# A paged-attention stage: the order of the key loads, a semaphore for the new keys, and their scaling moved from VectorE to GpSimd

## The chip, the cores and the metric

The kernel runs on one core of one Trainium2 chip. The metric is the device time of one execution in microseconds (us). TensorE, VectorE, ScalarE and GpSimd are the compute engines (PE, DVE, ACT and POOL in the profile); SyncE (SP) only issues DMAs.

## The reference

Two layers, each a conditioning block followed by a feed-forward block with LoRA experts and a residual. The block that matters here is the attention of the second layer: 64 batches (B) of 32 new tokens (S), 32 query heads, 8 key heads (HK), head size 128 (P), and 16 pages (NPP) of 32 cached keys each per batch.

```python
q = _rope(_rmsnorm(q, q_norm_w), pos); k = _rope(_rmsnorm(k, k_norm_w), pos)
kc = k_cache[block_table].reshape(bsz, L, HK, D)      # 512 cached keys per batch
k_all = jnp.concatenate([kc, k], axis=1)              # and 32 new ones
scores = jnp.where(valid, einsum('bqhd,bkhd->bhqk', q, k_all) * SCALE, -1e30)
o = einsum('bhqk,bkhd->bqhd', softmax(scores), v_all)
```

## The kernel before

The program goes through five stages: prologue, first feed-forward, `project` (queries, keys and values), `attention`, `output_projection`, then the second feed-forward. `project` stores turned but unnormalised keys (`qk_t`) and, apart from them, the reciprocal norms (`inv_d`, 8 heads x 32 tokens per batch). So the 32 new keys of a batch must be multiplied by their reciprocals in SBUF before they can be used.

`attention` is one software pipeline over units; a unit is one key head of one batch, so a batch has 8. The helper `turns` unrolls the first 12 steps and then loops over 16 units (two batches) at a time. At step u each engine works on several units at once; `live(n)` marks the part of the step that belongs to unit u - n. I number the steps of a batch 0 to 7, step 0 being the one at which its first unit enters. For a batch b the order is:

- VectorE, step 1 (`live(1)`): waits for all keys of b (`s_kp[q]`), multiplies the new ones by `inv` (line 1454), counts `s_fixed`. This stands ahead of the last split of batch b - 1 in the same step.
- VectorE, steps 2 and 3 (`live(2)`, `split`): the high half of the keys of the first two heads (line 1444, waits for `s_fixed`), then the low half (line 1447), which counts `s_lo`. In each step the splits stand ahead of the masked scores and row maxima of an older unit (line 1467).
- TensorE, step 4 (`live(4)`): the scores of unit 0 (line 1354), which wait for `s_lo`. TensorE works strictly in this order: scores, turning of probabilities (1363), products with cached values (1388), and once in four steps those with new values (1395). The last 1395 of batch b - 2 stands in step 0 of batch b and counts `s_nw`.
- GpSimd, once a batch: waits for `s_nw` of batch b - 2, copies the factors of b (line 1330), copies its row numbers (1311), issues four indirect DMAs that gather the cached values of b (1305).
- SyncE, once a batch: queries, then, when the key buffer is free (`s_lo` of the last split of b - 2), the reciprocals (1236), 16 pages (1245), the new keys (1248), then new values (1253) and the store of results.

All key buffers (`kt`), value buffers and so on are double: `q` is the parity of the batch. Batches 0 and 1 are prepared by `project`: its VectorE part multiplies their new keys (line 1031) after waiting for all 17 loads of the batch (line 1030), and only then starts the attention's own VectorE program, which computes the row numbers for the first gathers.

Of the kernel before, what the change touches and what calls it, by code (L numbers as in the profile page):

```python
# [19 lines left out]
ALU = mybir.AluOpType  # L20
# [3 lines left out]
P = 128  # L24
B, S, L = 64, 32, 512
# [5 lines left out]
HQ, HK, D = 32, 8, 128  # L31
REP = HQ // HK
PAGES, PSIZE, NPP = 64, 32, 16
# [672 lines left out]
def wait_apart(eng, sem_passed, *waits):  # L706


    for sem, v in waits:
        wait(eng, sem, v)  # L710
    eng.sem_inc(sem_passed, 1)
# [84 lines left out]
def project(nc, block, sems, ps, dram, cst, xh, xl, tables, spare, wcol, shared, qk_t, v_own, k_t, sums_d, ksums_d, inv_d, w, keys, first, early, spent):  # L796
# [6 lines left out]
    with ExitStack() as ctx:  # L803
        sb = lambda n, s, d=F32: ctx.enter_context(nc.sbuf_tensor("pr_" + n, s, d))
        sem = lambda n: sems.enter_context(nc.semaphore("pr_s_" + n))
        kt, qk, s_kp, s_qk = keys
        s_ev, s_xlo, s_tab = first
        turned = sb("turned", [P, 2, 2, 512])
        sums = sb("sums", [P, 512])
# [55 lines left out]
        @block.sync  # L865
        def _(e):
            src = bass.AP(tensor=dram["itok_Bx16_0_63"].tensor, offset=0, ap=[[0, 1], [1, 2 * NPP]])
            e.dma_start(page[0:1, :], src).then_inc(s_page, 16)

            def store(i, j):  # L870
                c, p, q = chunk(i, j), pair(i, j), j // 2 % 2
                high, n, _ = split(j)
                for half in range(2):
                    for head in range(2):
                        at = c * P + (2 * head + high) * S
                        cols = slice(at, at + S) if static(at) else bass.ds(at, S)
                        e.dma_start(qk_t[n * NT:(n + 1) * NT, half * H:(half + 1) * H, cols].rearrange("b d x -> d b x"),
                                    turned[head * H:(head + 1) * H, q, half, :].rearrange("p (b x) -> p b x", b=NT)).then_inc(s_qs[q], 16)

            def step(i, j, u, live):  # L880
                if live(0) and j % NT == 0 and not (static(u) and u == 0):
                    w.load(e, chunk(i, j) + 1, chunk(i, j) + 1)
                if live(2) and j % 2 == 1:
                    e.wait_ge(s_rot, pair(i, j - 2) + 1)
                    store(i, j - 2)
                if live(4) and (j - 4) % PER == PER - 1:
                    it = i + (j - 4) // PER
                    e.wait_ge(s_cs, it + 2)
                    for n in range(T // 512):
                        rows = slice(it * 8, it * 8 + 8) if static(it) else bass.ds(it * 8, 8)  # L890
                        out = ksums_d[n:n + 1, :, :] if key(u - 4) else sums_d[n:n + 1, rows, :]
                        e.dma_start(out.rearrange("o h x -> (o h) x"), sums[n * 32:n * 32 + 8, :]).then_inc(s_cd, 16)

            steps(e, step)
            for c, t, n in values:
                n -= QKT
                if t == 0 and c + 1 < chunks:
                    w.load(e, c + 1, c + 1)
                e.wait_ge(s_stage, n + 1)
                staged, s_stored, _ = staging(n)  # L900
                e.dma_start(v_own[t * P:(t + 1) * P, (c - NQU) * 512:(c - NQU + 1) * 512], staged).then_inc(s_stored, 16)
                b, place = divmod(n, NPP)
                if n == 0:
                    e.wait_ge(s_page, 16)
                if place == 2:
                    for q in range(2):
                        e.wait_ge(*rotated[q])
                    e.dma_start(kt[:, b, NPP, :],
                                qk_t[b:b + 1, :, HK * P:HK * P + HK * S].rearrange("o d x -> (o d) x")).then_inc(s_kp[b], 16)
                    e.dma_start(qk[:, b, :], qk_t[b:b + 1, :, 0:HK * P].rearrange("o d x -> (o d) x")).then_inc(s_qk[b], 16)  # L910
                if place % PPT == 0:
                    at = b * NPP + place
                    pages = nc.values_load_multi_w_load_instructions(
                        page[0:1, at:at + PPT], engines=[mybir.EngineType.SP], min_val=0, max_val=PAGES - 1,
                        skip_runtime_bounds_check_because="the block table holds numbers of pages of the cache")[1]
                e.dma_start(kt[:, b, place, :], k_t[bass.ds(pages[place % PPT] * P, P), :]).then_inc(s_kp[b], 16)
                if n == 4:
                    e.wait_ge(s_cd, 64 * (QKT // PER + 1))
                    e.dma_start(roots[:, :], sums_d.rearrange("n h x -> (n h) x")).then_inc(s_ss, 16)
                    e.dma_start(roots_k[:, :], ksums_d.rearrange("n g x -> (n g) x")).then_inc(s_ss, 16)  # L920
                if n == 14:
                    e.wait_ge(s_inv, 1)
                    for m in range(T // 512):
                        e.dma_start(inv_d[m * NT:(m + 1) * NT, :, :].rearrange("b g s -> g b s"),
                                    roots_k[m * HK:(m + 1) * HK, :].rearrange("g (b s) -> g b s", s=S)).then_inc(s_id, 16)
                if n == 17:
                    e.wait_ge(s_id, 64)
                    e.dma_start(sums[:, :], inv_d[0:2, :, :].rearrange("(o b) g s -> o (b g s)", o=1).broadcast_to([P, 512])).then_inc(s_id, 16)
                if c == chunks - 1 and t == 6:
                    e.wait_ge(w.s_lo, chunks * KB)  # L930
                    early.load(e, dram)
# [53 lines left out]
        def _(e):  # L985
# [41 lines left out]
            e.wait_ge(s_id, 80)  # L1027
            for b in range(2):
                new = kt[:, b, NPP, :]
                e.wait_ge(s_kp[b], 16 * (NPP + 1))  # L1030
                e.tensor_tensor(new, new, sums[:, b * HK * S:(b + 1) * HK * S], ALU.mult).then_inc(s_fixed, 1)
            e.wait_ge(s_fixed, 2)

# [142 lines left out]
def attention(nc, block, sems, ps, dram, cst, k_t, qk_t, v_own, o_t, inv_d, ri_d, keys, results, early, projected, late):  # L1176
# [7 lines left out]
    PER = 2 * UB  # L1184
    CB = T // 512
    QU = REP
    NPG = NPP + 1
    W = 2 * P
    SC = 1.0 / math.sqrt(D)
    with ExitStack() as ctx:  # L1190
        sb = lambda n, s, d=F32: ctx.enter_context(nc.sbuf_tensor("at_" + n, s, d))
        sem = lambda n: sems.enter_context(nc.semaphore("at_" + n))
        kt, qk, s_kp, s_qk = keys
        w_raw, o_raw, ri_b, s_w, s_or, s_on, s_ot = results
        s_proj, s_stage, s_rot, rotated, stores, own_stored = projected
        tiles, own = (NQU + HK // REP) * NT, HK // REP * NT
# [31 lines left out]
        def _(e):  # L1228
# [4 lines left out]
            def load_keys(b, q):  # L1233

                scales = inv_d[bass.ds(b, 1), :, :] if not isinstance(b, int) else inv_d[b:b + 1, :, :]
                e.dma_start(inv[:, q, :], scales.rearrange("o g s -> o (g s)").broadcast_to([P, HK * S])).then_inc(s_kp[q], 16)

                for n in range(0, NPP, PPT):
                    at = b * NPP + n
# [3 lines left out]
                        skip_runtime_bounds_check_because="the block table holds numbers of pages of the cache")  # L1243
                    for k in range(PPT):
                        e.dma_start(kt[:, q, n + k, :], k_t[bass.ds(numbers[k] * P, P), :]).then_inc(s_kp[q], 16)
                cols = slice(HK * P, HK * P + HK * S)
                src = qk_t[bass.ds(b, 1), :, cols] if not isinstance(b, int) else qk_t[b:b + 1, :, cols]
                e.dma_start(kt[:, q, NPP, :], src.rearrange("o d x -> (o d) x")).then_inc(s_kp[q], 16)

            def load_v(b, q):  # L1250
                own = v_own[bass.ds(b * S, S), :] if not isinstance(b, int) else v_own[b * S:(b + 1) * S, :]
# [50 lines left out]
        def _(e):  # L1302
# [5 lines left out]
            def indices(b, q):  # L1308

                cols = slice(b * KC, (b + 1) * KC) if isinstance(b, int) else bass.ds(b * KC, KC)  # L1310
                e.tensor_copy(idx[:, q, :], rows[:, cols]).then_inc(s_idx, 1)

            e.wait_ge(s_rot, NQU * NT // 2)
            e.wait_ge(s_rows, 1)
            for q in range(2):
# [4 lines left out]
            e.memset(v_new[0][:, :, :], 0.0).then_inc(s_cleared_rs, 1)  # L1320
            e.wait_ge(s_proj, tiles)
            e.memset(v_new[1][:, :, :], 0.0).then_inc(s_cleared_rs, 1)
            e.wait_ge(s_factors, 1)
            for q in range(2):
                e.tensor_copy(factor[:, q, :], factors[q][:, 0:HK]).then_inc(s_factor, 1)
            with e.Fori(0, B // 2 - 1) as i:
                for q in range(2):
                    b = i * 2 + q
# [2 lines left out]
                    indices(b + 2, q)  # L1331
                    wait_apart(e, s_passed[0], (s_idx, b + 3))
                    gather_values(q)

        @block.tensor
        def _(e):
# [67 lines left out]
        def _(e):  # L1404
# [14 lines left out]
            def step(i, j, u, live):  # L1419
# [14 lines left out]
                        ins.then_inc(s_ri, 1)  # L1434
                def split(jj):
                    q, g, w = (jj // UB) % 2, jj % UB, (jj // 2) % 2
                    if g == 0 and not (isinstance(u, int) and jj < PER):
                        e.wait_ge(s_fixed, i * 2 + jj // UB - 1)
                    elif g == 0:
                        e.wait_ge(s_kp[q], 16 * NPG)  # L1440
                    two = lambda x: x[:, w, :, :].rearrange("p x (n k) -> p n x k", k=PSIZE)
                    raw = kt[:, q, :, (g // 2) * 2 * PSIZE:(g // 2 + 1) * 2 * PSIZE].rearrange("p n (x k) -> p n x k", k=PSIZE)
                    if g % 2 == 0:
# [3 lines left out]
                        e.tensor_tensor(two(k_lo), raw, two(k_hi).bitcast(F32), ALU.subtract).then_inc(s_lo, 1)  # L1447


                if live(1) and (j - 1) % UB == 0 and not (isinstance(u, int) and j - 1 < PER):  # L1450
                    q = (j - 1) // UB % 2
                    new = kt[:, q, NPP, :]
                    e.wait_ge(s_kp[q], (i + (j - 1) // PER) * 16 * (NPG + 1) + 16 * NPG)
                    e.tensor_tensor(new, new, inv[:, q, :], ALU.mult).then_inc(s_fixed, 1)
                if live(2) and not (isinstance(u, int) and u == 5):
                    split(j - 2)
                if isinstance(u, int) and u == 4:
# [268 lines left out]
def build(nc, dram, out_t):  # L1726
# [12 lines left out]
    with ExitStack() as ctx:  # L1739
# [12 lines left out]
        kt = shared[:, 0:KT_SIZE].rearrange("p (q n x) -> p q n x", q=2, n=NPP + 1)  # L1752
        qk = shared[:, KT_SIZE:KT_SIZE + QK_SIZE].rearrange("p (q x) -> p q x", q=2)
        pair = lambda n: [ctx.enter_context(nc.semaphore(f"{n}{q}")) for q in range(2)]
        keys = kt, qk, pair("s_kp"), pair("s_qk")
        place = nc.sbuf_base
        with ExitStack() as sems:
            sb = lambda c, n, s, d=F32, side=None: c.enter_context(nc.sbuf_tensor(n, s, d, side=side))
# [96 lines left out]
```

## Time and profile before

| | |
|---|---|
| median of 3 runs | 2443.51 us (2442.0 to 2443.9) |
| profiled execution, time and span | 2442.34 us, 2440.2 us |
| busy share of the span | PE 96%, DVE 75%, ACT 50%, POOL 21% |
| mean granted TensorE clock | 0.986 of full |

The span runs from the first to the last instruction of the profiled execution. The attention pipeline lies between about 722 and 2015 us of it.

### The profile page before, as it was taken

The page shows a single profiled execution, that of the slowest core. Times are in us where ns is not written, and L with a number is a line of the kernel's source. Part 1 is how long each engine was busy: PE and PEld are TensorE (multiplying, and loading weights), DVE is VectorE, ACT ScalarE, POOL GpSimd, SP SyncE. Part 2 cuts the span into 40 slices and gives each one's busy share as a digit, 9 for nine tenths or more (in the row PEclk, how much of TensorE's full clock was granted, in tenths as well). Part 3 has the DMA queues.
Part 4 walks back from the last instruction along what each step waited for, and adds up shares of the span by engine and source line. Part 5 has one row for each costly group of instructions (what it writes and reads, how often), then busy time and mean ns, then how long its engine had stood idle before and what let it go on. Part 6 is the DMA issues. An engine that isn't in the chain of part 4 may idle for free. (4 is left out here: it accounts for less than half of the span.)

```text
span 2440.2 us, 50026 instructions
## 1 busy us (share of the span) xinstructions
PE 2330.8 (96%) x15564; PEld 2111.2 (87%) x15564; DVE 1822.9 (75%) x3082; ACT 1229.0 (50%) x2424; POOL 512.5 (21%) x537
## 2 busy tenths in 40 slices
PE   5999999999979999999999999999999999999999
PEld 4887777777859999999999999999999998888877
DVE  6659889889417877878787788787777787666654
ACT  3334444444316666666666666666666672111120
POOL 0002222222011222222222222222222214122100
PEclk8999999999989999999999999999999999999999
DMA  9845665566656888887878888888787888666522
GB/s 338 267 133 109 112 123 111 111 125 112 173 177 217 281 287 282 281 296 266 290 269 280 284 278 278 288 282 291 266 288 265 287 299 278 212 219 223 202 91 104
DMA packets 693166, 553.58 MB, mean 227 GB/s; under 512 B 369300, under 2 KB 608180, under 8 KB 688500
## 3 DMA queue, kind: packets, MB, share of 16 engines
q1 hardware_dynamic: 650628, 409.66, 54.3%
q0 software_dynamic: 36864, 134.23, 16.2%
q10 hardware_dynamic: 5616, 8.93, 1.1%
q8 instruction: 34, 0.56, 0.1%
q14 instruction: 24, 0.20, 0.0%
HBM read 449.17 MB, written 101.40 MB: 226 GB/s over the span
## 5 line engine op out<-in xcount | busy, mean ns | idle before, releaser
L1388 PE MATMUL ps<-at_pt,at_v_raw 128*128 128x128 f32 x4096 | 546.4, 277 | 0.0
L1467 DVE CUSTOM_DVE_ANT_0 at_sm<-ps,at_mask,at_factor 128x544 f32<-128x544 f32 x512 | 399.7, 781 | 149.6 <-PE ps L1354 105.7
L1388 PEld LDWEIGHTS ps<-at_pt,at_v_raw 128*128 128x128 f32 x4096 | 503.1, 194 | 0.0
L1540 ACT ACTIVATE at_pr<-at_sm,at_nm 128x544 f32<-128x544 f32 x512 | 384.4, 751 | 174.2 <-DVE at_nm L1467 162.1
L1527 ACT ACTIVATE at_pt<-ps 128x512 f32<-128x512 f32 x512 | 304.8, 595 | 261.8 <-PE ps L1363 190.1
L1354 PE MATMUL ps<-at_k_hi,at_q_hi 128*128 128x256 f32 (+1 forms) x1024 | 258.2, 333 | 74.2 <-DVE at_k_lo L1447 50.2
L1447 DVE TENSOR_TENSOR at_k_lo<-shared,at_k_hi 128x1088 fp32r<-128x1088 f32 x256 | 327.3, 1279 | 0.0
L1305 POOL DMA_INDIRECT at_v_raw<-v_cache,at_idx x256 | 290.7, 1136 | 113.5 <-issue 62.4
L1363 PE MATMUL ps<-constants,at_pr 128*128 128x128 f32 x2048 | 309.9, 274 | 0.0
L790 PE MATMUL ps<-xh,pr_hi 128*128 128x512 f32 x640 | 251.3, 393 | 0.0
L792 PE MATMUL ps<-xl,pr_hi 128*128 128x512 f32 x640 | 249.1, 389 | 0.0
L791 PE MATMUL ps<-xh,pr_lo 128*128 128x512 f32 x640 | 249.0, 389 | 0.0
L1363 PEld LDWEIGHTS ps<-constants,at_pr 128*128 128x128 f32 x2048 | 245.6, 141 | 0.4
L1354 PEld LDWEIGHTS ps<-at_k_hi,at_q_hi 128*128 128x128 f32 x1024 | 157.8, 194 | 87.3 <-issue 86.7
L953 ACT ACTIVATE spare<-ps,norm_columns 128x512 f32<-128x512 f32 x160 | 110.4, 690 | 235.5 <-PE ps L792 235.4
L1354 PE MATMUL ps<-at_k_hi,at_q_lo 128*128 128x256 f32 (+1 forms) x1024 | 214.3, 291 | 0.0
L1354 PE MATMUL ps<-at_k_lo,at_q_hi 128*128 128x256 f32 (+1 forms) x1024 | 213.8, 290 | 0.0
L1712 PE MATMUL ps<-op_ohi,op_whi 128*128 128x512 f32 x512 | 199.3, 389 | 0.0
L1713 PE MATMUL ps<-op_ohi,op_wlo 128*128 128x512 f32 x512 | 199.2, 389 | 0.0
L1655 ACT ACTIVATE op_ohi<-o_raw 128x2048 fp32r<-128x2048 f32 x31 | 59.5, 1921 | 268.4 <-PE ps L1717 250.3
L1444 DVE CAST at_k_hi<-shared 128x1088 fp32r<-128x1088 f32 x256 | 194.0, 758 | 0.0
L1330 POOL COPY at_factor<-at_factors 128x8 f32 x62 | 18.6, 300 | 833.6 <-PE ps L1395 833.6
(250 smaller groups left out, 3937.2 us busy)
## 6 DMA issues: line engine op xcount, KB each, us to landing
shared<-k_t SPq DMA_DIRECT2D x1024, 128.0 KB
qk_t<-pr_turned SPq DMA_DIRECT2D x320, 128.0 KB, 2.5
shared<-qk_t SPq DMA_DIRECT2D x64, 512.0 KB, 7.1
o_t<-at_ot SPq DMA_DIRECT2D x64, 512.0 KB
o_raw<-o_t SPq DMA_DIRECT2D x32, 1024.0 KB, 5.4
shared<-ri_d SPq DMA_DIRECT2D x32, 1024.0 KB, 7.9
f_w<-wqkv SPq DMA_DIRECT2D x12, 1024.0 KB, 5.6
s_k_in<-k_cache SPq DMA_DIRECT2D x16, 512.0 KB, 7.5
```

The source lines that it names most:

```text
L790: e.matmul(out, hi, xh[:, k, cols], start=(k == 0), stop=False)
L791: e.matmul(out, lo, xh[:, k, cols], start=False, stop=False)
L792: last = e.matmul(out, hi, xl[:, k, cols], start=False, stop=(k == KB - 1))
L1305: e.indirect_dma_start(out=v_raw[:, q, c, :], out_offset=None, in_=dram["v_cache"], in_offset=bass.IndirectOffsetOnAxis(ap=idx[:, q, c:c + ...
L1354: last = e.matmul(scores(r)[:, part], a, b[:, w, g % 2, part], start=first, stop=end)
L1363: last = e.transpose(ps_w(jj % 2)[:, c * P:(c + 1) * P], pr[:, w, k, c * P:(c + 1) * P], ident)
L1388: e.matmul(sums(w, k), v_raw[:, q, c, g * D:(g + 1) * D], pt[:, jj % 4, c * P:(c + 1) * P], start=(k == 0 and c == 0), stop=False, skip_gr ...
L1447: e.tensor_tensor(two(k_lo), raw, two(k_hi).bitcast(F32), ALU.subtract).then_inc(s_lo, 1)
L1467: e.tensor_tensor_reduce(out=sm[:, r, :], in0=scores(r), in1=mask[:, q, :], scale=factor[:, q, g:g + 1], scalar=3e38, op0=ALU.add, op1=ALU ...
L1527: e.activation(pt[:, jj % 4, :], ps_w(jj % 2), ACT.Copy).then_inc(s_pt, 1)
L1540: e.activation(pr[:, w, k, :], sm[:, r, :], ACT.Exp, bias=nm[:, at], scale=-1.0, accum_out=su[:, at]).then_inc(s_e, 1)
L1712: e.matmul(out, w_hi[par][:, r, cols], o_hi[q][:, r, :], start=(r == 0), stop=False)
```

## The change

Three edits. In `load_keys` the new keys are asked for right after the reciprocals, ahead of the 16 pages, and both count on a new pair of semaphores `s_kn`; `s_kp` counts the pages alone. The multiplication by the reciprocals leaves VectorE's step 1 and goes to GpSimd, at the end of its work for the batch, behind the four gathers; VectorE waits for the pages at the first split instead. And GpSimd's first two copies of factors move ahead of the first gathers. In `project`, line 1030 waits for the new keys alone.

```diff
@@ project, VectorE
             for b in range(2):
                 new = kt[:, b, NPP, :]
-                e.wait_ge(s_kp[b], 16 * (NPP + 1))
+                e.wait_ge(s_kn[b], 16)
                 e.tensor_tensor(new, new, sums[:, b * HK * S:(b + 1) * HK * S], ALU.mult).then_inc(s_fixed, 1)
@@ attention, SyncE, load_keys
-                e.dma_start(inv[:, q, :], scales.rearrange("o g s -> o (g s)").broadcast_to([P, HK * S])).then_inc(s_kp[q], 16)
+                e.dma_start(inv[:, q, :], scales.rearrange("o g s -> o (g s)").broadcast_to([P, HK * S])).then_inc(s_kn[q], 16)
+                cols = slice(HK * P, HK * P + HK * S)
+                src = qk_t[bass.ds(b, 1), :, cols] if not isinstance(b, int) else qk_t[b:b + 1, :, cols]
+                e.dma_start(kt[:, q, NPP, :], src.rearrange("o d x -> (o d) x")).then_inc(s_kn[q], 16)
                  for n in range(0, NPP, PPT):
...
-                cols = slice(HK * P, HK * P + HK * S)
-                src = qk_t[bass.ds(b, 1), :, cols] if not isinstance(b, int) else qk_t[b:b + 1, :, cols]
-                e.dma_start(kt[:, q, NPP, :], src.rearrange("o d x -> (o d) x")).then_inc(s_kp[q], 16)
@@ attention, GpSimd
+            e.wait_ge(s_factors, 1)
+            for q in range(2):
+                e.tensor_copy(factor[:, q, :], factors[q][:, 0:HK]).then_inc(s_factor, 1)
             e.wait_ge(s_rot, NQU * NT // 2)
...
             e.memset(v_new[1][:, :, :], 0.0).then_inc(s_cleared_rs, 1)
-            e.wait_ge(s_factors, 1)
-            for q in range(2):
-                e.tensor_copy(factor[:, q, :], factors[q][:, 0:HK]).then_inc(s_factor, 1)
             with e.Fori(0, B // 2 - 1) as i:
...
                     gather_values(q)
+                    new = kt[:, q, NPP, :]
+                    wait_apart(e, s_passed[0], (s_kn[q], i * 32 + 48))
+                    e.tensor_tensor(new, new, inv[:, q, :], ALU.mult).then_inc(s_fixed, 1)
@@ attention, VectorE
                 def split(jj):
+                    if g == 0:
+                        e.wait_ge(s_kp[q], (i + jj // PER + 1) * 16 * NPP)
                     if g == 0 and not (isinstance(u, int) and jj < PER):
                         e.wait_ge(s_fixed, i * 2 + jj // UB - 1)
-                    elif g == 0:
-                        e.wait_ge(s_kp[q], 16 * NPG)
...
-                if live(1) and (j - 1) % UB == 0 and not (isinstance(u, int) and j - 1 < PER):
-                    q = (j - 1) // UB % 2
-                    new = kt[:, q, NPP, :]
-                    e.wait_ge(s_kp[q], (i + (j - 1) // PER) * 16 * (NPG + 1) + 16 * NPG)
-                    e.tensor_tensor(new, new, inv[:, q, :], ALU.mult).then_inc(s_fixed, 1)
```

## Rows read from the trace of the kernel before

**Rows 1.** Head of the page: the span.
```profile
span 2440.2 us, 50026 instructions
```
**Rows 2.** Waits in 760 to 1990 us: total, times, longest (us).
```profile
POOL at_factor L1330 <- PE ps L1395: 833.6, 62, 27.4
...
DVE shared L1454 <- DMA shared<-qk_t: 117.3, 54, 4.0
...
PE ps L1354 <- DVE at_k_lo L1447: 40.2, 42, 2.7
```
**Rows 3.** Timeline of VectorE, one batch: start, us, engine, line [idle before].
```profile
1403.68 0.43 DVE L1454 TENSOR_TENSOR shared<-shared,at_inv 128x256 f32<-128x256 f32 x1 [1.80 <-DMA shared<-qk_t]
1404.02 1.29 DVE L1447 TENSOR_TENSOR at_k_lo<-shared,at_k_hi 128x1088 fp32r<-128x1088 f32 x1
...
1405.92 0.78 DVE L1444 CAST at_k_hi<-shared 128x1088 fp32r<-128x1088 f32 x1
...
1407.99 1.28 DVE L1447 TENSOR_TENSOR at_k_lo<-shared,at_k_hi 128x1088 fp32r<-128x1088 f32 x1
```
**Rows 4.** Timeline of GpSimd, the same batch and the start of the next.
```profile
1403.12 0.19 POOL L1330 COPY at_factor<-at_factors 128x8 f32 x1 [13.66 <-PE ps L1395]
...
1404.24 1.90 POOL L1305 DMA_INDIRECT at_v_raw<-v_cache,at_idx  x1 [0.81 <-POOL at_idx L1311]
...
1409.18 0.94 POOL L1305 DMA_INDIRECT at_v_raw<-v_cache,at_idx  x1 [0.30 <-issue]
1422.53 0.19 POOL L1330 COPY at_factor<-at_factors 128x8 f32 x1 [12.41 <-PE ps L1395]
```
**Rows 5.** Timeline of TensorE, the first scores of steps 1 to 4.
```profile
1402.61 0.49 PE L1354 MATMUL ps<-at_k_hi,at_q_hi 128*128 128x256 f32 x2
...
1405.44 0.52 PE L1354 MATMUL ps<-at_k_hi,at_q_hi 128*128 128x256 f32 x2 [0.50 <-DVE at_k_lo L1447]
...
1407.65 0.49 PE L1354 MATMUL ps<-at_k_hi,at_q_hi 128*128 128x256 f32 x2
...
1409.73 0.50 PE L1354 MATMUL ps<-at_k_hi,at_q_hi 128*128 128x256 f32 x2
```
**Rows 6.** Single lines of GpSimd, whole span: min/median/max ns, first to last start.
```profile
L1330 POOL COPY at_factor<-at_factors x62: 187/188/1305, 761.0 to 1983.0; 128x8 f32 x62
L1305 POOL DMA_INDIRECT at_v_raw<-v_cache,at_idx x256: 933/1013/2071, 719.4 to 1989.1; - x128
L1052 POOL TENSOR_TENSOR shared<-shared x80: 1302/1305/1838, 172.0 to 625.0; 128x512 f32<-128x512 f32 x80
```
**Rows 7.** SyncE's issues for the next batch's keys: start, us.
```profile
1409.68 9.76 SPq L1245 DMA_DIRECT2D shared<-k_t  x16
1419.64 0.33 SPq L1248 DMA_DIRECT2D shared<-qk_t  x1
```
**Rows 8.** TensorE around 1085 us: timeline, then windows (PEclk is third from the end).
```profile
1083.77 0.51 PE L1354 MATMUL ps<-at_k_hi,at_q_hi 128*128 128x256 f32 x2 [2.35 <-DVE at_k_lo L1447]
...
1086.64 0.80 PE L1354 MATMUL ps<-at_k_hi,at_q_hi 128*128 128x256 f32 x2
...
1089.66 0.50 PE L1354 MATMUL ps<-at_k_hi,at_q_hi 128*128 128x256 f32 x2
...
1085.10:1088.50 3.40, 3.40 (x19) 3.40 (x17) 2.51 (x4) 1.62 (x6) 0.67 (x1) 0.52 1.00 397
...
716.50:740.40 23.90, 8.85 (x38) 8.59 (x39) 13.10 (x26) 3.89 (x9) 12.21 (x14) 0.50 0.61 199
```
**Rows 9.** Timeline at the start of the attention.
```profile
715.47 0.42 DVE L1031 TENSOR_TENSOR shared<-shared,pr_sums 128x256 f32<-128x256 f32 x1 [34.61 <-DMA shared<-k_t]
...
722.01 0.79 PE L1354 MATMUL ps<-at_k_hi,at_q_hi 128*128 128x256 f32 x2 [10.02 <-DVE at_k_lo L1447]
...
733.67 0.79 DVE L1467 CUSTOM_DVE_ANT_0 at_sm<-ps,at_mask,at_factor 128x544 f32<-128x544 f32 x1 [9.41 <-POOL at_factor L1325]
...
734.61 0.79 PE L1354 MATMUL ps<-at_k_hi,at_q_hi 128*128 128x256 f32 x2 [9.54 <-DVE at_nm L1467]
```

More of the change, by code:

```diff
@@ L805, in project @@
         sem = lambda n: sems.enter_context(nc.semaphore("pr_s_" + n))
-        kt, qk, s_kp, s_qk = keys
+        kt, qk, s_kp, s_kn, s_qk = keys
         s_ev, s_xlo, s_tab = first
@@ L908, in _ @@
                     e.dma_start(kt[:, b, NPP, :],
-                                qk_t[b:b + 1, :, HK * P:HK * P + HK * S].rearrange("o d x -> (o d) x")).then_inc(s_kp[b], 16)
+                                qk_t[b:b + 1, :, HK * P:HK * P + HK * S].rearrange("o d x -> (o d) x")).then_inc(s_kn[b], 16)
                     e.dma_start(qk[:, b, :], qk_t[b:b + 1, :, 0:HK * P].rearrange("o d x -> (o d) x")).then_inc(s_qk[b], 16)
@@ L1186, in attention @@
     QU = REP
-    NPG = NPP + 1
     W = 2 * P
@@ L1192, in attention @@
         sem = lambda n: sems.enter_context(nc.semaphore("at_" + n))
-        kt, qk, s_kp, s_qk = keys
+        kt, qk, s_kp, s_kn, s_qk = keys
         w_raw, o_raw, ri_b, s_w, s_or, s_on, s_ot = results
@@ L1754, in build @@
         pair = lambda n: [ctx.enter_context(nc.semaphore(f"{n}{q}")) for q in range(2)]
-        keys = kt, qk, pair("s_kp"), pair("s_qk")
+        keys = kt, qk, pair("s_kp"), pair("s_kn"), pair("s_qk")
         place = nc.sbuf_base
```

## The prediction

> **What bounds the kernel now.** I read the head of the page first (the span is 2440.2 us [rows 1], against 2442.3 us of the execution, so 2.1 us lie around it), then the waits of the attention loop, since the change touches nothing else. VectorE waits 117.3 us in 54 of 62 batches at line 1454 for a key DMA, up to 4.0 us at a time; TensorE waits only 40.2 us for a low half of keys; GpSimd waits 833.6 us for the last line 1395 of a batch [rows 2]. So TensorE bounds, with a small leak from the late keys, and GpSimd has much idle time. But that idle time lies ahead of line 1330, and this is what decides here: GpSimd is idle because it may not start a batch's work before TensorE has finished with the value buffer, and the change puts the multiplication behind that wait.
>
> Next the timelines of one batch. Let t be the time from the start of line 1330, which is 1403.12 us here [rows 4]. 62 starts between 761.0 and 1983.0 us give a mean period of 1222.0 / 61 = 20.03 us [rows 6]. TensorE begins the scores of step 1 at t = -0.51, waits 0.50 us in front of step 2, begins step 4 at t = 6.61, and the next 1330 comes at t = 19.41 [rows 4, 5]. Steps without a wait are 2.08 us (1407.65 to 1409.73) or 2.21 us (1405.44 to 1407.65), so without a wait step 2 begins at -0.51 + 2.08 = 1.57 and step 4 at 1.57 + 2.21 + 2.08 = 5.86. From step 4 to the next 1330 it takes 19.41 - 6.61 = 12.80 us of plain TensorE work. A batch without any wait takes 18.66 us, and the leak is 20.03 - 18.66 = 1.37 us a batch, 85 us over the 62.
>
> **The change part by part.** Batches 2 to 63 go through the loop: 62 times each.
>
> *Removed from VectorE:* line 1454, 0.43 us, and its wait in step 1 [rows 3]. The last split of the older batch then starts up to 1.80 us earlier, so step 2 of TensorE no longer waits. Alone this could return at most the 85 us above.
>
> *Load order:* the same 18 DMAs; the new keys go ahead of 9.76 us of page issues, each page moves back by the 0.33 us of the new keys' issue [rows 7]. The last transfer lands about when it did, but it is needed at the first split of step 2, not at step 1, and the period becomes longer (below). I cost it at nothing. If that cover were gone, the old wait would stand in step 2 instead. The queries ahead and the new values and store behind them in SyncE's queue keep their place.
>
> *Added to GpSimd:* the multiplication of step 2's keys. It is issued behind: factor copy, row numbers, four gathers. The first gather starts at t = 1.12 [rows 4]; four at the median of 1.013 us [rows 6] with three gaps of 0.30 end at t = 1.12 + 4.05 + 0.90 = 6.07. In this batch they end at 7.00 [rows 4], because VectorE worked beside them; in the changed kernel VectorE will stand still then, so I take the medians. The trace has no such product on GpSimd. The nearest row is line 1052, twice as long, at 1305 ns [rows 6]; from below 0.65 us (half of it), from above 1.84 us (its longest). With a fixed part of 0.19 us, the small copy of line 1330, it is 0.19 + 1.115 / 2 = 0.75 us, which I take. The gap ahead of it lies between the 0.30 and the 0.81 us ahead of the gathers; I take 0.30, since its own wait (`s_kn`) was met long before. So the new keys are ready at t = 6.07 + 0.30 + 0.75 = 7.12.
>
> The Trainium skill (GPSIMD Engine Reference, Engine selection) puts two-input elementwise work on GpSimd at about twice VectorE's time. Twice the 0.43 us would be 0.86 us and the sum 7 us higher; it speaks against the move, but not for its main cost.
>
> *The wait this creates.* VectorE's split at 1444 waits for `s_fixed`. In this batch it started at t = 2.80 [rows 3, 4]; now it starts at 7.12 + 0.05 = 7.17. Queued behind it are 1467 of an older unit, the low query half and 1447: from the start of 1444 to the end of that 1447 it is 1407.99 + 1.28 - 1405.92 = 3.35 us [rows 3], so 10.52. TensorE's step 4 follows 0.13 us after the end of a 1447 (1404.02 + 1.29 to 1405.44) [rows 3, 5], at 10.65. TensorE has only steps 1 to 3 to do before it, done by 5.86. **It idles about 4.8 us a batch**, and since GpSimd starts only at TensorE's step 0, nothing catches up. The period is 10.65 + 12.80 = 23.45 us, 3.42 more than now: 62 x 3.42 = 212 us.
>
> *The clock.* Around 1085 us TensorE had idled 2.35 us; just behind it the granted clock was 0.52 for 3.4 us, its lower level of 1.2 GHz, and two steps took 1083.77 to 1089.66 = 5.89 us instead of 2.21 + 2.08 = 4.29: 1.60 us lost. And at the start of the attention, in a stretch with 8.85 us of work in 23.9, it was 0.50 throughout [rows 8]. A 4.8 us idle in every batch should bring such a stretch each time, and it falls in the 12.80 us that TensorE bounds: 62 x 1.60 = 99 us.
>
> The Trainium skill has the same pattern (TensorE: Matmul & The Clock Gate, HAM oscillation): a wait in each round of a loop sends the clock down and it is paid again every round. By that rule the 99 us come in full; without it the sum would be 99 us lower. The trace agrees for single idles, none as regular as this.
>
> *The start of the attention, once.* VectorE waited 34.61 us in line 1031 for pages that the multiplication does not need [rows 9]; on `s_kn` it goes on at once, so row numbers, first gathers and first splits are done while `project` still multiplies. TensorE's 10.02 us wait at 722.01 goes. The 9.41 us of VectorE for the factors, and with it TensorE's 9.54 us, goes because the copies stand ahead of the gathers. Together 19.6 us: I take -20. From below nothing, if another input (new values, row numbers) is as late; from above 23.9, the whole slow stretch.
>
> *Sum:* 2442.3 + 212 + 99 - 20 = 2733 us for the profiled execution, which was 1.2 under the median: **2735 us**.
>
> **The rivals.**
>
> *A: the stall, but no slow clock.* Against it: the 0.52 and 0.50 of [rows 8]. For it: the loop has more idles, 42 waits of TensorE for 1447 [rows 2], and the mean clock stayed at 0.986. 2735 - 99 = 2636 us; with the gathers at the shortest (933 ns) and the product at 0.65 the period is 23.0 and the time 2610.
>
> *B: deeper.* Gathers ending at 7.00, a gap of 0.81, a product of 1.84: step 4 at 7.00 + 0.81 + 1.84 + 0.05 + 3.35 + 0.13 = 13.18, period 25.98, 62 x 5.95 = 369: 2442 + 369 + 99 - 20 = 2890. Or two slow stretches a batch: 2735 + 99 = 2834.
>
> *C: faster.* The multiplication is in time after all and the leak is gone: 2443.5 - 85 - 20 = 2338 us. This needs `s_fixed` before VectorE reaches the first split, t about 2.8 at the latest that costs nothing now, and with TensorE's slack (5.86 instead of 10.65) at most t = 7.12 - 4.79 = 2.3. The first gather starts at 1.12 and four follow [rows 4]: it would have to overtake them. Its program order forbids this.
>
> *D: the wait only moves.* The pages are as late at the first split as the new keys were at 1454, GpSimd hides behind them: some 2423 us, the start's gain alone. It too needs t below about 3.
>
> **How the numbers follow.** Forecast 0.74; A 0.15; B 0.06; C 0.03; D 0.02, of which half within 0.2%. The range reaches over the forecast and most of A to its side and to two slow stretches on the other: 2625 to 2840. 0.2% (5 us) is what a measurement of this kernel can tell from no change. Faster 0.04, same 0.01, slower 0.95.
>
> **What would show it.** Right: line 1454 gone from VectorE and a product of about 0.75 us on GpSimd that ends some 7 us after 1330; VectorE idle in front of 1444 until GpSimd, over 4 us, 62 times; TensorE idle 4 to 5 us ahead of one 1354 a batch for 1447; period 23.5 to 25; a mean clock near 0.9; TensorE's first scores near 713 us with no wait for factors. Wrong: 1444 released by a DMA, a period under 20, or a clock that stays at 0.98. The sum fails most easily in the clock, then in how long GpSimd's product and the gap ahead of it take.

## The result

The changed kernel takes 2727.53 us (median of 4, 2725.77 to 2729.44) against 2443.16 us (median of 4) for the kernel before: ratio 1.1165, 95% interval 1.1145 to 1.1184. It is 11.7% slower. 2735 us were forecast.

The profile after, first its page: the span and busy times, and the granted clock over the 40 slices.

```profile
span 2725.6 us, 50181 instructions
...
PE 2433.9 (89%) x15564; PEld 2215.3 (81%) x15564; DVE 1799.7 (66%) x3020; ACT 1235.3 (45%) x2424; POOL 502.9 (18%) x599
...
PEclk8999999999998899899889898988998899999999
```

PE fell from 96% to 89% and is still longer busy, 2434 us against 2331: the same matmuls, a part of them at the lower clock. The waits of the loop, total, times and longest, as in [rows 2]:

```profile
DVE at_k_hi L1446 <- POOL shared L1335: 327.2, 62, 7.1
...
PE ps L1356 <- DVE at_k_lo L1449: 252.7, 62, 5.9
```

VectorE no longer waits for a DMA in the loop (117.3 us in [rows 2]); it waits for GpSimd, in each of the 62 batches, and TensorE waits 252.7 us for VectorE where it waited 40.2. (Lines moved: 1330, 1444, 1447, 1354, 1395 and 1305 of before are 1329, 1446, 1449, 1356, 1397 and 1304 now; the product is 1335.)

One batch, engine by engine, in the views of [rows 3 to 5]. GpSimd:

```profile
1488.87 0.19 POOL L1329 COPY at_factor<-at_factors 128x8 f32 x1 [19.15 <-PE ps L1397]
...
1489.99 1.00 POOL L1304 DMA_INDIRECT at_v_raw<-v_cache,at_idx  x1 [0.81 <-POOL at_idx L1310]
...
1493.80 0.94 POOL L1304 DMA_INDIRECT at_v_raw<-v_cache,at_idx  x1 [0.31 <-issue]
1494.76 0.73 POOL L1335 TENSOR_TENSOR shared<-shared,at_inv 128x256 f32<-128x256 f32 x1
1513.43 0.19 POOL L1329 COPY at_factor<-at_factors 128x8 f32 x1 [17.94 <-PE ps L1397]
```

VectorE:

```profile
1495.60 0.76 DVE L1446 CAST at_k_hi<-shared 128x1088 fp32r<-128x1088 f32 x1 [5.23 <-POOL shared L1335]
...
1497.57 1.28 DVE L1449 TENSOR_TENSOR at_k_lo<-shared,at_k_hi 128x1088 fp32r<-128x1088 f32 x1
```

TensorE, steps 3, 4 and 5:

```profile
1492.64 0.49 PE L1356 MATMUL ps<-at_k_hi,at_q_hi 128*128 128x256 f32 x2
...
1498.98 0.51 PE L1356 MATMUL ps<-at_k_hi,at_q_hi 128*128 128x256 f32 x2 [4.02 <-DVE at_k_lo L1449]
...
1503.60 0.50 PE L1356 MATMUL ps<-at_k_hi,at_q_hi 128*128 128x256 f32 x2
```

Read it from the top. With t counted from the start of 1329, as in the prediction, the gathers end at 5.87 and the product at 6.62. VectorE's split starts at 6.73 after 5.23 us of idling, its low half ends at 9.98, and TensorE's step 4 starts at 10.11. Step 4 to step 5 then takes 1503.60 - 1498.98 = 4.62 us; without a slow clock it is 3.00 us (shown below). The next 1329 comes at 24.56.

The window behind the idle, and the whole loop (PEclk third from the end):

```profile
1498.90:1502.30 3.40, 3.32 (x18) 3.32 (x19) 3.40 (x9) 2.12 (x5) 0.00 (x0) 0.62 0.92 305
...
740.00:2275.00 1535.00, 1282.34 (x9957) 1270.85 (x9957) 960.42 (x1907) 828.58 (x1784) 302.27 (x434) 0.91 0.66 226
```

Not every batch is like this one. Of the 61 periods 43 are 24.3 to 24.6 us long and 16 are 25.7 to 25.9 us; the other two, 27.2 and 27.5 us, hold the long gap told of at the end. In the longer ones the clock stays low into step 5 as well. One of them follows: step 4 takes 5.65 us and step 5 2.27, where the batch above has 4.62 and 2.08. Over 7.0 us the granted clock is 0.57:

```profile
824.60 0.82 PE L1356 MATMUL ps<-at_k_hi,at_q_hi 128*128 128x256 f32 x2 [4.00 <-DVE at_k_lo L1449]
830.25 0.69 PE L1356 MATMUL ps<-at_k_hi,at_q_hi 128*128 128x256 f32 x2
832.52 0.50 PE L1356 MATMUL ps<-at_k_hi,at_q_hi 128*128 128x256 f32 x2
```
```profile
824.60:831.60 7.00, 7.00 (x36) 7.00 (x37) 3.83 (x9) 2.77 (x6) 0.00 (x0) 0.57 1.04 338
```

The period over all batches, and the start of the attention, in the views of [rows 6] and [rows 9]:

```profile
L1329 POOL COPY at_factor<-at_factors x62: 188/188/192, 741.0 to 2261.9; 128x8 f32 x62
```
```profile
681.85 0.42 DVE L1031 TENSOR_TENSOR shared<-shared,pr_sums 128x256 f32<-128x256 f32 x1 [1.09 <-DMA shared<-qk_t]
...
712.52 0.41 PE L1356 MATMUL ps<-at_k_hi,at_q_hi 128*128 128x256 f32 x2
```

The mean period is (2261.9 - 741.0) / 61 = 24.93 us, 4.90 more than the 20.03 of [rows 6]; the first 1329 comes at 741.0 instead of 761.0. 62 x 4.90 - 20 = 284 us against 285.4 us between the two spans. All but 2 us of the difference is in these two terms.

### The profile page after: what moved, and what is told of

Same layout as the page of the kernel before. It is cut to its first block and busy times, and to the rows that moved or that the text cites. A ratio compares the mean times of both kernels' runs of the same rounds, so it can differ in the third digit from the quotient of the medians.

```text
span 2725.6 us, 50181 instructions
## 1 busy us (share of the span) xinstructions
PE 2433.9 (89%) x15564; PEld 2215.3 (81%) x15564; DVE 1799.7 (66%) x3020; ACT 1235.3 (45%) x2424; POOL 502.9 (18%) x599
## 5 line engine op out<-in xcount | busy, mean ns | idle before, releaser
L1390 PE MATMUL ps<-at_pt,at_v_raw 128*128 128x128 f32 x4096 | 584.1, 289 | 1.3 <-issue 1.3
L1390 PEld LDWEIGHTS ps<-at_pt,at_v_raw 128*128 128x128 f32 x4096 | 543.5, 207 | 1.5 <-issue 1.5
L1356 PE MATMUL ps<-at_k_hi,at_q_hi 128*128 128x256 f32 (+1 forms) x1024 | 270.7, 347 | 253.5 <-DVE at_k_lo L1449 252.7
L1356 PEld LDWEIGHTS ps<-at_k_hi,at_q_hi 128*128 128x128 f32 x1024 | 166.9, 205 | 265.7 <-issue 265.4
L1365 PE MATMUL ps<-constants,at_pr 128*128 128x128 f32 x2048 | 334.6, 290 | 0.0
L1304 POOL DMA_INDIRECT at_v_raw<-v_cache,at_idx x256 | 246.0, 961 | 113.4 <-issue 62.3
L1365 PEld LDWEIGHTS ps<-constants,at_pr 128*128 128x128 f32 x2048 | 264.5, 150 | 0.1
L1356 PE MATMUL ps<-at_k_hi,at_q_lo 128*128 128x256 f32 (+1 forms) x1024 | 224.4, 303 | 0.0
L1329 POOL COPY at_factor<-at_factors 128x8 f32 x62 | 11.7, 189 | 1140.7 <-PE ps L1397 1140.7
L1356 PE MATMUL ps<-at_k_lo,at_q_hi 128*128 128x256 f32 (+1 forms) x1024 | 222.2, 300 | 0.0
```

The lines of the kernel that those rows point to most:

```text
L1304: e.indirect_dma_start(out=v_raw[:, q, c, :], out_offset=None, in_=dram["v_cache"], in_offset=bass.IndirectOffsetOnAxis(ap=idx[:, q, c:c + ...
L1356: last = e.matmul(scores(r)[:, part], a, b[:, w, g % 2, part], start=first, stop=end)
L1365: last = e.transpose(ps_w(jj % 2)[:, c * P:(c + 1) * P], pr[:, w, k, c * P:(c + 1) * P], ident)
L1390: e.matmul(sums(w, k), v_raw[:, q, c, g * D:(g + 1) * D], pt[:, jj % 4, c * P:(c + 1) * P], start=(k == 0 and c == 0), stop=False, skip_gr ...
```

## The experiments

Times are compared by the ratio to the kernel before on the same chip, whose median was 2441.5 us (e1 to e4), 2436.7 us (e5, e6) and 2450.0 us (e7 to e10). A period is the time from the first to the last start of GpSimd's factor copy, divided by 61; the loop clock is the granted TensorE clock, taken over the loop.

### Where the product stands on GpSimd: e1, e2, e8, e3, e9

All five are the changed kernel with the product moved within GpSimd's work for the batch. e1 puts it ahead of the wait for TensorE, e2 ahead of the gathers:

```diff
 # e1
+                    new = kt[:, q, NPP, :]
+                    wait_apart(e, s_passed[0], (s_kn[q], i * 32 + 48))
+                    e.tensor_tensor(new, new, inv[:, q, :], ALU.mult).then_inc(s_fixed, 1)
                     wait_apart(e, s_passed[0], (s_nw, (b + 1) * 2))
                     e.tensor_copy(factor[:, q, :], factors[q][:, bass.ds(i * HK + HK, HK)]).then_inc(s_factor, 1)
                     indices(b + 2, q)
 # e2: the three lines stand here instead
                     wait_apart(e, s_passed[0], (s_idx, b + 3))
                     gather_values(q)
```

> GpSimd multiplies the new keys of a batch before it waits for TensorE's value buffer, instead of behind the gathers; all else as in the changed kernel. Theory (the place behind the gathers is what costs): TensorE's idle of 4.0 us a batch and the low clock behind it go, the period falls from 24.93 us to between 18.66 us (no wait at all) and 20.03 us, and with the gain of the start (20 us) the time is 2340 to 2425 us, faster than both kernels. Rival (GpSimd is too slow or collides with VectorE at this product wherever it stands): VectorE still waits for it at the first split and the time stays above 2500 us. Second rival (the pages are as late as the new keys were): the period stays at 20.0 and the time is about 2423 us.

> The product stands behind GpSimd's wait for TensorE and its two small copies, but ahead of the four gathers. Theory: ready at t = 0.32 + some 0.1 + 0.73 = 1.2 us after the start of the factor copy, before VectorE reaches its first split at 1.4 to 2.8, so no new wait: within 5 us of the variant with the product ahead of the wait. Rival (the wait for TensorE's step 0 itself is what costs, whatever stands behind it): still over 2600 us.

e8, e3 and e9 gather in two parts, n gathers, the product, 4 - n gathers:

```diff
-                    gather_values(q)
+                    gather_values(q, range(n))     # e8: n = 1, e3: n = 2, e9: n = 3
                     new = kt[:, q, NPP, :]
                     wait_apart(e, s_passed[0], (s_kn[q], i * 32 + 48))
                     e.tensor_tensor(new, new, inv[:, q, :], ALU.mult).then_inc(s_fixed, 1)
+                    gather_values(q, range(n, KC))
```

> One gather, the product, three gathers. By the same sum as for two and four gathers ahead: product ends at 1.12 + 0.95 + 0.02 + 0.73 = 2.82, step 4 at 2.82 + 3.49 = 6.31 against 5.86 without a wait, period 19.1 us: 2442 - 57 - 20 = 2365 us, near the variants with the product first. Rival (any gather ahead shows in full): 62 x 1.25 = 78 us less than with two ahead, 2375 us, or more.

> Two gathers, the product, two gathers. Theory (each gather ahead of the product delays the split by its 0.95 us and its gap of 0.30): product ends at t = 1.12 + 2 x 0.95 + 0.30 + 0.73 = 4.07, step 4 of TensorE begins at 4.07 + 0.11 + 3.25 + 0.13 = 7.56, TensorE idles 1.7 us less the modelled overlap of its matmul ends, period 7.56 + 12.80 = 20.36 us and few slow stretches of the clock: 2442 + 62 x 0.33 - 20 = 2443 us, up to 2500 if each idle still brings a slow stretch. Rival (a fixed price of the hand-over between GpSimd and VectorE, not the gathers): about 2700 us.

> Three gathers, the product, one gather. Product ends at 1.12 + 3 x 0.95 + 2 x 0.30 + 0.73 = 5.30, step 4 at 8.79, period 21.6 us without the clock: 2442 + 62 x 1.56 - 20 = 2519 us. TensorE idles some 2.7 us. If each such idle brings a slow stretch (1.6 to 2.0 us), up to 2640 us; if none does, 2519 us.

| product stands | period, us | loop clock | time, us | ratio to before (95%) |
|---|---|---|---|---|
| ahead of the wait (e1) | 18.96 | 1.00 | 2357.25 | 0.9648 (0.9624 to 0.9673) |
| ahead of the gathers (e2) | 19.03 | 1.00 | 2361.62 | 0.9663 (0.9639 to 0.9687) |
| behind 1 gather (e8) | 19.17 | 1.00 | 2369.19 | 0.9667 (0.9643 to 0.9692) |
| behind 2 (e3) | 20.47 | 1.00 | 2453.24 | 1.0045 (1.0030 to 1.0060) |
| behind 3 (e9) | 22.82 | 0.95 | 2593.21 | 1.0578 (1.0551 to 1.0604) |
| behind 4 (the change) | 24.93 | 0.91 | 2727.53 | 1.1165 (1.1145 to 1.1184) |

The times of e8 and e3 lie 4 and 10 us above their forecasts, and e9's lies in its range of 2519 to 2640 us. The rivals of e1 and e2 fall: GpSimd is fast enough for this product, and the wait for step 0 costs next to nothing by itself. The first gather is all but free. VectorE does wait for the product in e8, 1.4 us a batch, but TensorE is still busy with steps 1 to 3 for most of that time:

```profile
1491.31 0.76 DVE L1447 CAST at_k_hi<-shared 128x1088 fp32r<-128x1088 f32 x1 [1.44 <-POOL shared L1335]
...
1492.14 0.49 PE L1357 MATMUL ps<-at_k_hi,at_q_hi 128*128 128x256 f32 x2
1494.70 0.51 PE L1357 MATMUL ps<-at_k_hi,at_q_hi 128*128 128x256 f32 x2 [0.24 <-DVE at_k_lo L1450]
```

Step 3 takes 2.56 us here instead of 2.08. In return step 5 takes 2.08 (medians over the batches); in e1 it takes 2.39, because step 6 waits there for a low half that VectorE has late (its 1449 ends at 1510.67, step 6 starts at 1510.80). From the second gather on each costs its length and gap, 20.47 - 19.17 = 1.30 us for the second. The third costs 2.35 us, more than its 1.25, and e9's timeline shows why. TensorE's steps 4 and 5 of one batch, then the starts of three batches on GpSimd:

```profile
1023.67 0.51 PE L1357 MATMUL ps<-at_k_hi,at_q_hi 128*128 128x256 f32 x2 [2.73 <-DVE at_k_lo L1450]
1028.27 0.50 PE L1357 MATMUL ps<-at_k_hi,at_q_hi 128*128 128x256 f32 x2
```
```profile
1038.10 0.19 POOL L1329 COPY at_factor<-at_factors 128x8 f32 x1 [16.28 <-PE ps L1398]
1061.40 0.19 POOL L1329 COPY at_factor<-at_factors 128x8 f32 x1 [16.32 <-PE ps L1398]
1083.04 0.19 POOL L1329 COPY at_factor<-at_factors 128x8 f32 x1 [14.66 <-PE ps L1398]
```

Periods of 23.3 us (a slow step 4, 4.60 us) and 21.6 us stand side by side, the second being the 21.6 that was expected without the clock. The same idle of 2.7 us brings the lower clock in 41 of the 61 periods and leaves it at 1.00 in the other 20. With two gathers ahead the idle is 1.5 us and the clock of the loop is 1.00.

e1 is the fastest kernel of this study, 3.5% under before. Its GpSimd, one batch:

```profile
1495.73 0.73 POOL L1330 TENSOR_TENSOR shared<-shared,at_inv 128x256 f32<-128x256 f32 x1 [8.88 <-DMA shared<-qk_t]
1499.62 0.19 POOL L1332 COPY at_factor<-at_factors 128x8 f32 x1 [3.15 <-PE ps L1397]
```

GpSimd now waits for the new keys and for TensorE one after the other, both in time that it has; the product ends 3.15 us ahead of the factor copy.

### What the clock costs: e5 and e7

Both add matmuls of a constant tile, which no output uses, while TensorE would idle in step 4 (a row counts each of them twice: 18 stand as x36). e5 put 18 of them right ahead of the wait for `s_lo`, e7 16 ahead of every wait of the step, in a bank that is free there:

```diff
 # e7
                 if live(4):
                     m, jj = u - 4, j - 4
                     g, q, r, w = jj % UB, (jj // UB) % 2, jj % 2, (jj // 2) % 2
+                    if g == 0 and not (isinstance(u, int) and jj < PER):
+                        e.wait_ge(s_pt, u - 7)
+                        for _ in range(16):
+                            e.matmul(ps[:, 4, 0:P], ident, ident, start=True, stop=True)
```

> The changed kernel, with 18 matmuls of a constant tile (128x128, f32, into an unused part of a score bank) ahead of TensorE's wait in step 4 of every batch from the third on; they add work that no output uses and take some 18 x 0.20 = 3.6 us of the 4.0 us idle. Theory (62 slow stretches of the clock cost 2.0 us a batch, 125 us): granted clock back to 0.98 or more, period from 24.93 to about 22.9 us, time about 2605 us. Rival (what follows the wait is long for another reason, such as work that VectorE and ScalarE must catch up): the clock rises, the period stays at 24.9 us and the time at 2727 us.

> As the first run with extra matmuls, but they stand ahead of every wait of step 4, in a bank of the turned probabilities that is free then, and are 16: some 16 x 0.22 = 3.5 us of the 4.0 us idle. The first ones had stood behind a wait for VectorE's low query half and so ran late and in full view. Theory (the slow stretches of the clock cost the 2.0 us a batch between 24.93 and 10.11 + 12.80 = 22.91 us): clock 0.98 or more, period 22.9 us, time 2727 - 125 = 2602 us, although TensorE does 16 more matmuls a batch. Rival (another reason for the long stretch behind the wait): period stays near 24.9, time near 2727 us.

e5 took 2878.98 us, ratio 1.1812 (1.1792 to 1.1832), where about 2605 us were expected. It missed, and it doesn't decide between its theory and its rival. Its matmuls stood behind the wait for the low query half, which VectorE makes after the very split that is late; TensorE idled 2.73 us first, then ran them in view:

```profile
1493.52 5.91 PE L1351 MATMUL ps<-constants 128*128 128x128 f32 x36 [2.73 <-DVE at_q_lo L1499]
```

e7 took 2614.35 us, ratio 1.0664 (1.0636 to 1.0691) against 1.1165 of the changed kernel. That is 111 us less by the two spans and 122 us by the ratios, although TensorE does more. TensorE, then the window of step 4:

```profile
1489.50 3.74 PE L1348 MATMUL ps<-constants 128*128 128x128 f32 x32
1493.69 0.51 PE L1360 MATMUL ps<-at_k_hi,at_q_hi 128*128 128x256 f32 x2 [0.45 <-DVE at_k_lo L1453]
...
1496.69 0.49 PE L1360 MATMUL ps<-at_k_hi,at_q_hi 128*128 128x256 f32 x2
```
```profile
1493.60:1497.00 3.40, 3.31 (x28) 3.31 (x29) 3.40 (x9) 2.28 (x5) 0.00 (x0) 1.00 1.00 313
```

The clock is 1.00 where it was 0.62, step 4 takes 3.00 us instead of 4.62, and the period is (2150.7 - 746.0) / 61 = 23.03 us, close to the 22.91 expected. VectorE's wait for GpSimd is untouched (327.1 us in 62 batches). The rival falls: what stood behind the idle was the clock. Of the 12 us missing to the forecast 2602, 7 are in the period, most of them in the two batches with the long gap. The other 5 lie ahead of the first factor copy, at 746.0 instead of 741.0. The edit puts the extra matmuls into batches 1 to 62, and in batch 1 TensorE has no idle to fill, so they stand in full view: the scores ahead of them start at 727.51 and the next at 733.16, 5.65 us for a step that takes 2.08 without them.

```profile
729.67 3.74 PE L1348 MATMUL ps<-constants 128*128 128x128 f32 x32
733.16 0.50 PE L1360 MATMUL ps<-at_k_hi,at_q_hi 128*128 128x256 f32 x2
```

The first scores of the attention also start 1.1 us later, at 713.64 instead of 712.52, for which I have no reason.

### The other parts of the change: e4, e6, e10

e4 is the kernel before with only the start changed (`project` waits on `s_kn`; factor copies ahead of the first gathers; the loop's counts adapted). e6 is the changed kernel with the product given back to VectorE at step 1, waiting for the new keys alone. e10 is the changed kernel with the new keys asked for behind the pages again.

```diff
 # e6, VectorE
+                if live(1) and (j - 1) % UB == 0 and not (isinstance(u, int) and j - 1 < PER):
+                    q = (j - 1) // UB % 2
+                    new = kt[:, q, NPP, :]
+                    e.wait_ge(s_kn[q], (i + (j - 1) // PER) * 32 + 16)
+                    e.tensor_tensor(new, new, inv[:, q, :], ALU.mult).then_inc(s_fixed, 1)
```

> The loop as in the kernel before (load order, one semaphore, product on VectorE at step 1); only the start is changed: project waits for the new keys alone, and GpSimd copies the first factors ahead of its gathers. Theory: TensorE's two idles of 10.0 and 9.5 us at the start of the attention go and nothing else changes: 20 us faster, 2423 us. Rival (the start's gain is given back in the loop or was bought by the rest of the change): within 5 us of before.

> Load order, semaphores and start as in the changed kernel, but VectorE multiplies the new keys at step 1 as before, now waiting for them alone. Theory (the wait at step 1 was for the last DMA in the queue; the pages land in time for step 2): VectorE pays 0.43 us a batch that it can spare, its wait goes, time within 10 us of the variant with the product ahead of GpSimd's wait (2357 us). Rival (VectorE's 0.43 us counts in full): 27 us more, 2384 us. Second rival (the order changes nothing, the wait moves to the pages at step 2): 2420 us, as with the start alone.

> The changed kernel (product behind the gathers, semaphores apart) with one part undone: the new keys are asked for behind the 16 pages again. Theory (at a period of 24.9 us everything has landed long before GpSimd reaches the product): within 0.2% of the changed kernel, 2722 to 2733 us. Rival (the order matters here too): a wait of GpSimd for the DMA, over 2740 us.

e4: 2419.86 us, ratio 0.9901 (0.9869 to 0.9933), 22 us faster than its neighbours of before; its period is (1962.5 - 739.9) / 61 = 20.04 us, that of before. The start is worth its 20 us and touches nothing else.

e6: 2370.95 us, ratio 0.9728 (0.9712 to 0.9744), period (1912.0 - 741.7) / 61 = 19.19 us. So the load order, together with the semaphore that lets VectorE wait for the new keys alone, takes 0.85 us a batch off against e4, 53 us, with no work moved; the two weren't tried apart. Against e1 the period is 0.23 us longer, between the theory and the first rival. By what path the product on VectorE costs this is open: it stands in step 1, and the time is lost in step 5 (2.59 us against 2.39 in e1, medians). The pages were hardly late at the first split: VectorE waited for them in 13 batches, 5.3 us in all.

e10: 2724.94 us, ratio 1.1117 (1.1089 to 1.1145), period 24.91 us. In the changed kernel the order does nothing. Its list of waits has no engine that waits for a key DMA: in the long period the keys have landed before they are needed.

## Why the prediction was right

**The stall by program order: right.** GpSimd's product could not start before step 0 and four gathers; VectorE waited for it in 62 of 62 batches, TensorE for VectorE. e2 against the changed kernel shows it alone: four gathers moved from one side of the product to the other, 5.9 us of the period.

**Its size: 3.42 us a batch forecast, 2.88 measured.** Step 4 came at t = 10.11, not 10.65. Gathers ended at 5.87 (forecast 6.07). The median of before was the wrong row for a VectorE that stands still: 181 of its 256 gathers ran beside a busy VectorE. Here each takes 0.94 to 1.00 us. The gap ahead of the product was 0.02 us, not 0.30. The product took 0.73 us (0.75 was scaled from the 128x512 row), and VectorE's four operations 3.25 us (3.35). 62 x 0.54 = 33 us too much.

**The clock: 1.60 us a batch forecast, 2.02 measured** (24.93 less 10.11 + 12.80). The term was taken from the one case of [rows 8]; e7 shows that it is the clock. The price of one slow stretch was right: in the 43 shorter periods it is 24.50 - 22.91 = 1.59 us. What was wrong is that each batch would have one such stretch: in the 16 periods of 25.8 us it is nearly twice as dear, 2.9 us. With the two long gaps that makes the 62 x 0.42 = 26 us too little. The Trainium skill's rule of a loop that pays for its wait every round (TensorE: Matmul & The Clock Gate, HAM oscillation) held at this idle of 4.0 us, where the clock fell in all 61 periods. At 2.7 us it held in 41 of 61 (e9), at 1.5 us in none (e3). The two errors nearly cancel, so that the total came within 8 us is partly luck.

**The start: -20 forecast, -20.0 measured** (741.0 against 761.0), and e4 gives it by itself.

**Load order at nothing: right here** (e10), with the cover that the prediction named. It also said that with this cover gone the old wait would stand in step 2; that was wrong. With the cover gone, in e6, only 5.3 us of it stand there, and the order with its semaphore gains 53 us, most of the 85 us leak that the prediction read off.

**The rivals.** A (no slow clock, 2636 us) is what e7 makes by hand, 2614 us. B's first form (2890 us) did not come, since none of its three long terms did. Its second, two slow stretches a batch, came in part, in the 16 long periods. C (2338 us) did not come, as the program order ahead of the product forbids it; once the product stands ahead of the wait, e1 comes to 2357 us: 66 of the 85 us leak. The other 19 are the 0.31 us a batch of e1's step 5, a wait that the prediction's wait-free batch of 18.66 us left out. D (the wait only moves) fell with e6. The bound read off for C, a product ready by t = 2.3, falls between e8 (product ends at 2.85, 0.2 us of period lost) and e2 (1.05).

The Trainium skill (GPSIMD Engine Reference, Engine selection) advises against two-input work on GpSimd at about twice VectorE's time. The traces say 0.73 us against 0.43, 1.7 times, and still e1 beats e6 by 0.23 us a batch (the two ratios' intervals lie apart): a slower engine with free time may do it, if the work stands where that time is.

## What to carry to other kernels

An engine's idle time is not one pool: ask at which wait it idles, and on which side of that wait and of the engine's own queue the new work stands. Here the same product costs nothing that shows ahead of the wait and 6 us of every 25 behind the gathers. When a stall falls on TensorE in each round of a loop, add what the clock does behind it: a stall of 4.0 us cost 6. And split a change before judging it: of this one the start (-20 us) and the load order with its semaphore (-53 us) were good, and one line's place hid both.

## What the runs showed of the hardware

With one idle of TensorE in each round of the loop, the loop's clock was 1.00 at 1.5 us of idle (e3), 0.95 at 2.7 us with slow and fast rounds mixed (e9), and 0.91 at 4.0 us. Filling 3.7 of 4.2 us with useless matmuls brought it back to 1.00 and made the kernel at least 111 us faster. The length of an idle alone doesn't decide: two single idles of 3.4 us in e3 left the clock at 1.00, while 2.7 us lowered it in 41 of 61 periods of e9. What else decides is not shown.

```profile
1282.52 0.52 PE L1357 MATMUL ps<-at_k_hi,at_q_hi 128*128 128x256 f32 x2 [3.43 <-DVE at_k_lo L1450]
...
1282.40:1289.40 7.00, 6.88 (x59) 6.89 (x60) 5.90 (x13) 4.64 (x10) 0.00 (x0) 1.00 1.03 380
```

An indirect gather's time on GpSimd goes with what VectorE does beside it: median 1013 ns before [rows 6], 941 ns here, where VectorE stands still during most of them. The 191 gathers of the changed kernel beside an idle VectorE took at most 0.96 us; the 181 of before beside a busy one had a median of 1.13 us and took up to 2.07.

```profile
L1304 POOL DMA_INDIRECT at_v_raw<-v_cache,at_idx x256: 934/941/1806, 698.4 to 2266.8; - x128
```

In two batches of the changed kernel the gap ahead of the second gather is 2.19 us instead of 0.30. Each of the twelve kernels has two such gaps, of 1.7 to 2.2 us, ahead of the same two of its 256 gathers, the 114th and the 226th. The reason is unknown:

```profile
1391.35 0.95 POOL L1304 DMA_INDIRECT at_v_raw<-v_cache,at_idx  x1 [2.19 <-issue]
...
2090.40 0.94 POOL L1304 DMA_INDIRECT at_v_raw<-v_cache,at_idx  x1 [2.19 <-issue]
```
